# One wait of the o_c load: the reciprocal's semaphore replaced by that of the normalisation

## The reference, cut to what matters

```
q = query @ wq + query @ Aq @ Bq * 4 ;  k = query @ wk ;  v = query @ wv + query @ Av @ Bv * 4
q, k = rope(q), rope(k)
scores = q @ k.T / sqrt(16), causal ;  attn = softmax(scores)
x = layernorm(query + (attn @ v) @ wo)
h = gelu(butterfly(x @ W_exp + b_exp, up) + up_bias)
y = butterfly(h, down) @ W_con + b_con + down_bias
x = layernorm(x + y)
```

## Time and profile before

| | |
|---|---|
| median of 3 executions | 1180.9 us |
| time of the profiled execution | 1180.9 us |
| its span (first to last instruction) | 1179.2 us |
| PE busy | 1091.7 us, 93% |
| DVE busy | 840.0 us, 71% |
| ACT busy | 674.4 us, 57% |
| POOL busy | 491.4 us, 42% |
| SP's DMA queue q1 | 166.53 MB, 51.2% of 16 engines' span |

### The profile page before, as it was taken

One profiled execution on the slowest core, in us unless ns is written; L12 is line 12 of the kernel. 1 busy time (PEld: TensorE's weight loads), 2 busy tenths in 40 slices (PEclk: granted clock), 3 DMA queues, 4 the chain that ended last, 5 costly groups with the idle time before them and its releaser, 6 DMA issues.

```text
span 1179.2 us, 27684 instructions
## 1 busy us (share of the span) xinstructions
PE 1091.7 (93%) x8462; PEld 791.5 (67%) x8462; DVE 840.0 (71%) x1951; ACT 674.4 (57%) x1067; POOL 491.4 (42%) x539
## 2 busy tenths in 40 slices
PE   4677699999999999999999999999999999999976
PEld 3454366767677776767677776767677777766665
DVE  6689867686868678686858678686858778676333
ACT  2277557474656657474656657474656658474601
POOL 5342524435363634435363634435353635433301
PEclk9678799999999999999999999999999999999989
DMA  7773553646465564646465564646465564641201
GB/s 267 162 214 88 167 131 102 185 111 195 93 213 127 182 156 132 174 110 197 95 206 127 182 159 134 169 109 203 93 203 127 181 162 138 166 116 49 74 28 36
DMA packets 94983, 169.90 MB, mean 144 GB/s; under 512 B 14872, under 2 KB 36120, under 8 KB 94944
## 3 DMA queue, kind: packets, MB, share of 16 engines
q1 hardware_dynamic: 93888, 166.53, 51.2%
q10 hardware_dynamic: 832, 1.83, 0.4%
q0 software_dynamic: 224, 1.04, 0.2%
HBM read 92.28 MB, written 77.07 MB: 144 GB/s over the span
## 4 chain that ended last, share of the span: by engine, by line
PE 76%; DVE 8%; DMA 8%; issue 3%; ACT 2%; POOL 1%; SPq 1%; DVEq 0%; POOLq 0%; ACTq 0%
PE ps_m L560 27%; PE ps_m L709 17%; PE ps_m L679 10%; PE ps_m L608 7%; PE ps_t L651 6%; PE ps_m L688 4%; DMA m_scr<-m_row 4%; DVE m_raw L905 2%; PE ps_m L637 2%; DMA q_st<-m_scr 2%; ACT pT L781 1%; DVE gact L991 1%; DVE y L991 1%; PE ps_m L671 1%; PE ps_m L694 1%
## 5 line engine op out<-in xcount | busy, mean ns | idle before, releaser
L781 ACT ACTIVATE pT<-ps_t 128x512 f32<-128x512 f32 x640 | 330.9, 602 | 223.1 <-PE ps_t L651 222.8
L905 DVE TENSOR_REDUCE m_raw<-ps_m 128x1 f32<-128x512 f32 (+2 forms) x768 | 338.6, 505 | 67.8 <-PE ps_m L637 62.3
L1046 POOL TENSOR_SCALAR_AFFINE_SELECT pT<-pT 128x512 f32<-128x512 f32 (+1 forms) x320 | 179.1, 562 | 450.3 <-ACT pT L781 447.4
L709 PE MATMUL ps_m<-w,gact 128*128 128x256 f32 x1024 | 231.6, 382 | 1.1 <-ACT gact L851 1.1
L709 PEld LDWEIGHTS ps_m<-w,gact 128*128 128x128 f32 x1024 | 191.9, 190 | 29.6 <-ACT gact L851 1.5
L608 PE MATMUL ps_m<-k_st,q_st 48*128 48x512 f32 (+3 forms) x1024 | 152.5, 354 | 26.3 <-DMA k_st<-qk_scr 15.1
L679 PE MATMUL ps_m<-pT,v_aug 128*32 128x512 f32 (+3 forms) x2048 | 157.9, 450 | 4.4 <-DVE m_raw L905 3.0
L608 PEld LDWEIGHTS ps_m<-k_st,q_st 48*128 48x128 f32 x1024 | 88.3, 189 | 84.6 <-issue 59.7
L651 PE MATMUL ps_t<-q_st,k_st 50*128 50x512 f32 (+3 forms) x1024 | 129.8, 354 | 12.8 <-DMA q_st<-m_scr 8.6
L952 DVE TENSOR_TENSOR y<-ps_m,y 128x256 f32<-128x256 f32 x64 | 27.2, 425 | 145.9 <-PE ps_m L709 145.9
L679 PEld LDWEIGHTS ps_m<-pT,v_aug 128*32 128x32 f32 x2048 | 58.8, 112 | 90.7 <-issue 78.8
(11 more groups left out here) (106 smaller groups left out, 1601.3 us busy)
## 6 DMA issues: line engine op xcount, KB each, us to landing
qk_scr<-rot_hi SPq DMA_DIRECT2D x64, 512.0 KB, 3.7
q_st<-qk_scr SPq DMA_DIRECT2D x128, 192.0 KB, 4.7
k_st<-qk_scr SPq DMA_DIRECT2D x128, 192.0 KB, 5.0
qk_scr<-rot SPq DMA_DIRECT2D x32, 512.0 KB, 4.0
o_scr<-o_raw SPq DMA_DIRECT2D x64, 256.0 KB, 3.0
r_b<-in_xT SPq DMA_DIRECT2D x17, 512.0 KB, 6.4
o_c<-o_scr SPq DMA_DIRECT2D x32, 256.0 KB
r_b<-r_scr SPq DMA_DIRECT2D x32, 256.0 KB
```

The lines of the kernel that those rows point to most:

```text
L709: mm = pe.matmul(pm[:, 0:D], gact[:, k, n * P:(n + 1) * P], w2[:, k, :], start=(k == 0), stop=(k == NHT - 1))
L781: act.activation(pT[:, g % 2, slot, half * T:(half + 1) * T], ps_t[:, ST_BANK[2 * n + r], :], ACT.Exp, scale=SCALE).then_inc(exp_done, 1)
L905: ins = dve.tensor_reduce(m_raw[:, r, u // 2, qt:qt + 1], scores[:, off:off + (qt + 1) * P], AX.X, ALU.max, negate=True)
L1046: pool.affine_select(out=v, in_=v, compare_op=ALU.is_ge, fill=0.0, base=0, pattern=pattern, channel_multiplier=-1).then_inc(mask_done, 1)
```

## The change

SMOC has three waits: until the raw outputs that it reads have landed (`raw_out`), until WO has read the batch that stood in `o_c` before (`done["WO"]`), and one for `s_m`. The last was a wait for RCPs: `rcp_done` at 2b + n says that the RCP before this one has read `s_m`. It is now a wait for ONs with the same value: `on_done` at 2b + n. For n = 0 that is both ONs of batch b - 1; for n = 1 it is also ON(b, 0), the multiplication of the same batch's first half.

```
                     hold(sp, raw_out, DMA * (NG * b + 2 * n + 2))
                     hold(sp, done["WO"], 2 * b)
-                    hold(sp, rcp_done, 2 * b + n)
+                    hold(sp, on_done, 2 * b + n)
                     both = o_scr[b, 2 * n:2 * n + 2, :, :].rearrange("g (h r) t -> (g h) r t", h=GH)
                     sp.dma_start(s_m[:, :], both[:, DH, :].rearrange("h (c t) -> h c t", c=8))\
                       .then_inc(sm_in, DMA)
```

## The result

The changed kernel takes 1255.05 us (median of 4 runs, 1248.9 to 1261.45) against 1183.34 us before (4 runs). The ratio is 1.061, 95% interval 1.054 to 1.068: slower by 6.1%, 72 us, where 33 us were forecast. The direction and the place were right; the size was not. The profiled execution took 1248.88 us with a span of 1247.1 us, 67.9 us more than the span before.

What follows compares the result with a forecast made beforehand. PE was taken to bound the kernel, busy for 65.3 of each 66.3 us period. 14 fill slips of 2.65 us, less 1.3 and 2.6, gave 33 us on top of 1180.9: 1214 us, range 1192 to 1230.

Steps and rivals of the forecast that it cites:

- n = 0 costs nothing, the tail and b = 14 next to nothing; SMOC(b,1) is released 4.15 us later: SMOC's new wait: already met for n = 0; for n = 1, s_m goes out 4.15 us later; tail keeps its length.
- Steps 1 and 2: SP's queue behind SMOC: QKH goes out 2.6 us later, REC 1.6 us later, and DVE loses nothing.
- Step 3: REC lands behind o_c and QKH traffic, so RB goes out 3.2 us later, or 2.6 at the lower end.
- Beside the path: RB's slip to ON(b,1) and WO: WO's 3.3 us cover is just used up, cost 0 to 0.1 us.
- Steps 4 to 6: QKL's traffic delays the m_scr write, FILL of group 0 slips 2.65 us, and PE's wait at ST number 15 grows equally.
- slack that was hardly there: Taken off the sum: 1.3 us for periods with slack, 2.6 us for the first static step.
- The sign that I had named for it: PE's waits on q_st<-m_scr, with those on k_st<-qk_scr, should grow from 8.6 to about 40 us in total.
- The clock stays at 1.00 in these stretches: PE's granted clock was to stay at 1.00 in the loop stretches where its waits grow.
- B: Rival: the small write isn't held by QKL's traffic, or o_c costs nothing; FILL slips less, 1197 us, chance 0.2.
- C: Rival: the delay is swallowed between SMOC and WO and by SP's idle 3.6 us; 1181 us, chance 0.07.
- D: Rival: faster, as traffic spreads and the block before m_scr thins out; at most to 1172 us, chance 0.04.
- A: Rival: the whole 4.15 us reach r_b and PE waits at WO; fills slip about 3.6 us; 1237 us, chance 0.08.

Runs made afterwards that it cites:

- e1: Changed kernel with the new wait for n = 0 only, n = 1 waiting for rcp_done as before: 1181.03 us, ratio 1.000.
- e7: Changed kernel with o_c issued ahead of the new wait, so that only s_m waits for ON(b,0): 1197.33 us, ratio 1.014.
- e4: Changed kernel with QKH(i+1,1) moved on SP behind RB(i-1,1), so that REC goes ahead of it: 1253.05 us.
- e9: Changed kernel with XTL(i+2), 512 KB, moved on SP ahead of MROW(i,2), its users unmoved: 1212.77 us, ratio 1.028.
- e11: Changed kernel with QKL(i+1,1) moved on SP to right behind REC(i-1,1), ahead of RB and XRES: 1215.45 us, ratio 1.030.
- e2b_warm4: Changed kernel with 4 thrown-away matrix products put on PE ahead of its wait for the row maxima at ST number 15: 1235.7 us.

## Why the prediction was wrong

- **n = 0 costs nothing, the tail and b = 14 next to nothing; SMOC(b,1) is released 4.15 us later.** Right: e1 gives 1.000, and `s_m` slips by 4.2 us. The loop's 4.96 us per period, 14 times, are 69.4 us, and the whole span grew by 67.9: nothing is left for the tail.
- **Steps 1 and 2 (QKH +2.6, REC +1.6, DVE loses nothing).** Right. DVE's busy time is the same, REC goes out at once when SP is free, 574.26.
- **Step 3 (RB slips by 3.2 us, 2.6 at the lower end).** Mis-sized: 4.0 at i = 7, 4.2 in the median. I added up the bytes as if the block stayed full until its end, and it ran out over 1.5 us. `o_c` ahead of QKH and REC costs 2.5 us of RB (e7), of which the sum had 0.9 for SP's issue and 0.8 for the bytes; without it the sum gives a slip of 1.5, as e7 has.
- **Beside the path: WO's cover of 3.3 us is just used up, cost 0 to 0.1.** Failed, as a result of step 3. With a slip of 4.0 WO waits 13 times for up to 2.1 us, 16.7 us in all. It is partly the same time as the later wait (e4 took it away and gained nothing), so it doesn't come on top of the fills' slip.
- **Steps 4 to 6 (FILL slips by 2.65 us, PE's wait by as much).** The mechanism is right, and shown by e9, e11 and e4. The size was not: FILL slipped by 3.1 at i = 7, within the stated 2.5 to 3.2, but by 3.4 in the median, and all waits together grew by 3.5 us per period. That is 49 us over 14 periods, where the sum had 37, less 3.9 for slack that was hardly there. This term, 14 x 2.65 - 3.9, was off by 16 us. The sign that I had named for it, waits for `m_scr` and `k_st` of about 40 us in total, did come true (39.5 + 2.7), but by luck: WO's 15.6 us more stand ahead of them in each step and took their share of the same delay.
- **"The clock stays at 1.00 in these stretches".** This is the step that failed outright. The sum had no term for what a wait does to the work behind it. It is 1.5 us per period and about 20 us in all (busy time; 16 to 19 us by e2b_warm4): a lower clock behind most of the waits at ST number 15, for 5.3 us at i = 7.
- **The rivals.** B, C and D are out. A had the right slip of RB and the wait at WO, and its 1237 us was nearer, but its place was wrong: without WO's wait the time stays (e4).

16 us of mis-sized waits and 20 of clock are the 36 to 39 us that were missing.

## What to carry to other kernels

Before a wait is added on an engine that issues DMAs, list what stands behind it in the queue, and follow the bytes: here a small DMA on which somebody waits landed when the last thin stretch of what was queued ahead had run out, later than the mean share and the bytes say. On a kernel in which PE is busy for 98% of a period, price new PE waits like these (2.1 to 3.3 us) with a second term for the lower clock behind them, here 40% on top of the waits. A large transfer should be put where the DMA engines are empty and nobody waits for a small one behind it: moving one of 512 KB was worth 42 us in the changed kernel and 2.7 us in the kernel before.

## What was not expected of the hardware

- Waits of PE of like length did not act alike. Behind 2.74 us the granted clock was 0.50 for 5.3 us; behind 2.87 us it stayed at 1.00. The runs of the changed kernel spread over 12.6 us (mean clocks of 0.930 to 0.942), those of the kernel before over 6.6 us. What tips it in a given period is not settled here.
- A transfer of 256 KB that uses 1.08 us of all DMA engines delayed the landing of a 16 KB write behind it by 2.5 us, with 1 MB between the two; 0.9 of that is the time that SP took to issue it.
- Work that is thrown away made the kernel faster: 4 products per period in a wait brought 19 us, while 9 of them, which overran the wait, gave nothing (7 us slower by the medians, with overlapping runs).
